# A transformer layer over 32 sequences on one core: another order of the calls in the steady turn and in the outer turns

## The reference

```python
mod = (silu(c) @ wmod).reshape(32, 6, 1, 128)      # sa, ca, ga, sb, cb, gb; ga and gb kept away from 0
h = layernorm(x) * (1 + ca) + sa
h = rmsnorm(h, norm_w)
q, k, v = h @ Wq, split(h @ Wkv)                   # 16 heads of 64, causal softmax over 256 keys
x = x + ga * ((sigmoid(h @ Wg) * softmax(mask(q @ k.T / 8)) @ v) @ Wout)
h = layernorm(x) * (1 + cb) + sb
# product-key experts: 4 heads, 2 x 64 keys, 8 best of each, 8 best of the 8 x 8 pairs, 512 experts
sim = einsum(h @ Wq2, keys); top8 of both halves; softmax over the 8 best pairs
w = silu(h . down_embed[idx]) * softmax; experts = sum(w * up_embed[idx])
mlp = (silu(h @ Wg2 + bg) * (h @ Wu + bu)) @ Wd + bd
x = x + gb * (mlp + experts)
```

## Time and profile before

| what | us |
|---|---|
| three timed runs | 1451.94, 1453.22 (median), 1456.62 |
| the profiled execution's own time | 1454.25 |
| its span, first to last instruction | 1452.5 |
| PE busy | 1400.9 (96%) |
| DVE busy | 1290.8 (89%) |
| ACT busy | 1265.5 (87%) |
| POOL busy | 1052.5 (72%) |

### The profile page before, as it was taken

How to read it: one execution, slowest core, us unless ns; L and a number is a source line. 1 busy time by engine, 2 the same in 40 slices (tenths; PEclk the granted TensorE clock), 3 DMA queues, 4 the chain that set the end, 5 groups by cost and what they waited for, 6 DMA issues and landing times.

```text
span 1452.5 us, 39813 instructions
## 1 busy us (share of the span) xinstructions
PE 1400.9 (96%) x11491; PEld 1163.0 (80%) x11491; DVE 1290.8 (89%) x5345; ACT 1265.5 (87%) x4194; POOL 1052.5 (72%) x1221
## 2 busy tenths in 40 slices
PE   6899999999999999999999999999999999999988
PEld 4678788888788888888888888888878888878868
DVE  6589999999999999999999999999999999999978
...
DMA packets 50753, 27.74 MB, mean 19 GB/s; under 512 B 10304, under 2 KB 49920, under 8 KB 50720
## 3 DMA queue, kind: packets, MB, share of 16 engines
...
...
## 4 chain that ended last, share of the span: by engine, by line
PE 79%; ACT 14%; issue 3%; DVE 2%; DMA 0%; SPq 0%; POOL 0%; ACTq 0%; DVEq 0%; POOLq 0%
PE pW L1381 9%; PE pS L1449 9%; PE pW L1462 9%; PE pW L1490 8%; PE pW L1383 8%; PE pW L1382 8%; PE pS L1439 7%; PE pS L1435 6%; PE pW L1530 4%; PE pW L1533 4%; ACT pS L644 4%; ACT pT L636 4%; PE pW L1466 3%; PE pW L1521 2%; ACT qk L626 2%
## 5 line engine op out<-in xcount | busy, mean ns | idle before, releaser
L644 ACT ACTIVATE pS<-pS,nmx 128x128 f32<-128x128 f32 (+1 forms) x1024 | 388.3, 433 | 34.7 <-DVE nmx L1031 34.7
L501 POOL TENSOR_TENSOR fexp<-fexp,fsum 128x512 f32<-128x512 f32 x240 | 299.8, 1281 | 76.9 <-DVE fexp L1145 76.9
L1031 DVE CUSTOM_DVE_ANT_0 pS<-pS,mask 128x128 f32<-128x128 f32 (+1 forms) x1024 | 331.6, 388 | 25.4 <-PE pS L1439 20.9
L636 ACT COPY pT<-pS 128x768 f32<-128x768 f32 x256 | 215.9, 843 | 40.9 <-PE pS L1449 38.5
L492 POOL TENSOR_TENSOR fsum<-ex 128x512 f32<-128x512 f32 x248 | 250.5, 1048 | 0.0
L1449 PE MATMUL pS<-ident,p_sb 128*128 128x128 f32 x1536 | 215.6, 277 | 5.3 <-DVE p_sb L1051 3.3
L1051 DVE TENSOR_TENSOR p_sb<-pS,coef 128x256 f32<-128x256 f32 (+2 forms) x512 | 210.5, 452 | 8.9
L1449 PEld LDWEIGHTS pS<-ident,p_sb 128*128 128x128 f32 x1536 | 173.3, 140 | 35.8 <-issue 19.6
L644 ACT ACTIVATION_READ_ACCUMULATOR pS<-pS,nmx 128x1 f32 x1024 | 194.7, 190 | 0.0
L626 ACT COPY qk<-pW 128x512 f32<-128x512 f32 x256 | 162.2, 634 | 5.9 <-PE pW L1383 2.3
L1462 PE MATMUL pW<-pT,v 128*64 128x256 f32 x1024 | 165.8, 402 | 0.3 <-ACT pT L636 0.2
...
## 6 DMA issues: line engine op xcount, KB each, us to landing
...
```

Source lines behind the costliest of these rows:

```text
L501: ins = nc.gpsimd.tensor_tensor(fexp[:, k, h, :], fexp[:, k, h, :], fsum[:, k, h].rearrange("p i j -> p (i j)"), ALU.mult)
L636: nc.scalar.copy(pT[:, p % 2], pS[:, p % 2, :, 0:SW]).then_inc(S(pT_ready), 1)
L644: ins = nc.scalar.activation(ps, ps, ACT.Exp, bias=nmx[:, p % 2, h, k:k + 1], scale=-1.0, accum_out=den(p)[:, h, k:k + 1])
L1031: ins = nc.vector.tensor_tensor_reduce(out=ps, in0=ps, in1=mask[:, (1 - k) * P:2 * P], scale=-1.0, scalar=LARGEST, op0=ALU.add, op1=ALU.mi ...
```

## The change

The same work is done in another order, on all engines. In the steady turn:

- PE: the table of banks and the list of calls are new. The turn begins with `project_qk(2)` instead of `project_v(0)`; `project_v(0)`, `project_v(3)` and two `project_qk` follow the first scores; `project_out` moves ahead of `transpose_scores(1)`; the two `project_down` are apart, one on each side of three score calls.
- ACT and DVE: lists to match. `rows2` stands ahead of `copy_transposes(2)`; `choose(1, 0)` follows the first `gate_product`, `choose(0, *)` stays.
- POOL: `add_bias` ahead of `weigh(0)`, `rstd2` ahead of `fold(0)`, `add_heads(1)` ahead of `rstd1`, `fold(1)` ahead of `rms1`.

In the outer turns: the first 256 columns of Wq and of Wkv are loaded first and split apart; the first layernorm's modulation is read straight from PSUM; the transposes of `down_embed` go from the start to the end of turn 0, and POOL splits that weight last; in the last turn the similarities are not shifted by DVE (`shift`), but ACT takes the exponentials from PSUM with the negated maximum as bias (`largest`, `expert_exp_last`), and several calls of the last turn change places.

The diff, cut to the steady lists and what the prediction speaks of:

```diff
...
+            sp.dma_start(w_qkv[:, 0:2 * P], Wq[:, 0:2 * P]).then_inc(load_pairs, 16)
+            sp.dma_start(w_qkv[:, DI:DI + 2 * P], Wkv[:, 0:2 * P]).then_inc(load_pairs, 16)
...
             sp.dma_start(key_sb[:, :, :], keys.rearrange("h k p n -> k h (p n)")).then_inc(load_keys, 16)
-            sp.dma_start(w_qkv[:, 0:DI], Wq).then_inc(load_q, 16)
-            sp.dma_start(w_qkv[:, DI:2 * DI], Wkv[:, 0:DI]).then_inc(load_k, 16)
-            sp.dma_start(down_sb[:, :, :], down.rearrange("(c p) d -> p c d", p=P)).then_inc(load_down, 16)
+            sp.dma_start(w_qkv[:, 2 * P:DI], Wq[:, 2 * P:DI]).then_inc(load_q, 16)
+            sp.dma_start(w_qkv[:, DI + 2 * P:2 * DI], Wkv[:, 2 * P:DI]).then_inc(load_k, 16)
             sp.dma_start(w_qkv[:, GV:GV + H], Wgate).then_inc(load_gv, 16)
             sp.dma_start(w_qkv[:, GV + H:], Wkv[:, DI:2 * DI]).then_inc(load_gv, 16)
+            sp.dma_start(down_sb[:, :, :], down.rearrange("(c p) d -> p c d", p=P)).then_inc(load_down, 16)
             sp.dma_start(w_out[:, :, :], Wout.rearrange("(j p) n -> p j n", p=P)).then_inc(load_w, 16)
             sp.dma_start(w_g[:, :], fWg).then_inc(load_w, 16)
...
@@ -580,16 +587,16 @@
                 candidates()
                 products(0)
                 products(1)
+                add_bias()
                 weigh(0)
-                add_bias()
                 add_heads(0)
+                rstd2()
                 fold(0)
-                rstd2()
                 weigh(1)
+                add_heads(1)
                 rstd1()
-                add_heads(1)
+                fold(1)
                 rms1()
-                fold(1)
             run(pool, body)
...
                             nc.scalar.activation(tops[:, :, :, :].rearrange("p a h n -> p (a h n)"), top_d[:, :, :, :].rearrange("p a h n -> p (a h n)"),
                                                  ACT.Exp).then_inc(S(tops_ready), 1)
+                def expert_exp_last(k):
+                    act.wait_ge(negated, k + 1)
+                    act.wait_ge(S(f_ready[k]), at(f_ready[k], g, 1))
+                    sim = w.bank("sim", k)[:, :].rearrange("p (a h n) -> p a h n", a=2, n=NK)
+                    for a in range(2):
+                        for h in range(RH):
+                            ins = nc.scalar.activation(ex[:, k, a * RH + h, :], sim[:, a, h, :], ACT.Exp, bias=neg[:, a, k * RH + h:k * RH + h + 1])
+                    w.release(ins, "sim", k)
+
+                def tops_exp():
+                    act.wait_ge(S(top_d_ready), at(top_d_ready, f, 1))
+                    act.wait_ge(S(cand_ready), at(cand_ready, g, 1))
+                    nc.scalar.activation(tops[:, :, :, :].rearrange("p a h n -> p (a h n)"), top_d[:, :, :, :].rearrange("p a h n -> p (a h n)"),
+                                         ACT.Exp).then_inc(S(tops_ready), 1)
...
+                queries(2)
                 copy_transposes(7, -1)
-                queries(2)
                 values(0)
+                values(3)
+                exp_scores(0)
                 queries(3)
-                exp_scores(0)
                 weighted(6)
-                values(3)
+                weighted(7)
+                queries(4)
                 gate_up(1)
+                copy_transposes(0, 0)
                 exp_scores(1)
-                weighted(7)
+                values(1)
+                scale_head(1)
+                queries(5)
+                exp_scores(2)
+                copy_transposes(1, 0)
                 down_tanh(0)
-                scale_head(1)
-                copy_transposes(0, 0)
+                total(0)
+                gate_up(2)
+                rows2()
+                weighted(0)
+                copy_transposes(2, 0)
+                exp_scores(3)
+                gate_up(3)
+                scale_head(3)
                 down_tanh(1)
-                copy_transposes(1, 0)
-                gate_up(2)
-                values(1)
-                exp_scores(2)
-                total(0)
-                weighted(0)
-                exp_scores(3)
-                copy_transposes(2, 0)
+                modulate_h()
+                copy_transposes(3, 0)
                 weighted(1)
-                queries(4)
-                scale_head(3)
-                rows2()
-                gate_up(3)
-                queries(5)
-                copy_transposes(3, 0)
-                values(4)
-                modulate_h()
                 high_part(h2T_high, h2T, "hT")
                 exp_scores(4)
                 queries(6)
-                weighted(2)
-                values(2)
+                values(4)
+                experts(0)
                 exp_scores(5)
                 queries(7)
-                values(5)
+                weighted(2)
+                weighted(3)
+                total(1)
                 scale_head(5)
-                weighted(3)
                 copy_transposes(4, 0)
                 copy_transposes(5, 0)
-                total(1)
+                values(2)
+                values(5)
+                expert_exp(0)
+                expert_exp(1)
+                experts(1)
+                rms_scale()
+                exp_scores(6)
                 weighted(4)
-                expert_exp(0)
-                rms_scale()
-                experts(0)
-                expert_exp(1)
                 high_part(xT_high, xT, "xT")
                 weighted(5)
-                experts(1)
-                exp_scores(6)
                 exp_scores(7)
                 gate_up(0)
+                copy_transposes(6, 0)
                 queries(0)
-                copy_transposes(6, 0)
                 scale_head(7)
                 queries(1)
...
+                def largest(k):
+                    w.wait_full("sim", k)
+                    sim = w.bank("sim", k)[:, :].rearrange("p (a h n) -> p a h n", a=2, n=NK)
+                    heads = slice(k * RH, (k + 1) * RH)
+                    apart()
+                    for a in range(2):
+                        for h in range(RH):
+                            ins = nc.vector.max(top_s[:, a, k * RH + h, :], sim[:, a, h, :])
+                    link(ins, head_chain, f)
+                    nc.vector.tensor_scalar(neg[:, :, heads], top_s[:, :, heads, 0], -1.0, None, ALU.mult).then_inc(negated, 1)
+                    if k == TB - 1:
+                        nc.vector.tensor_tensor(top_d[:, :, :, :], top_s[:, :, :, :], top_s[:, :, :, 0:1].broadcast_to([P, 2, TB * RH, TK]),
+                                                ALU.subtract).then_inc(S(top_d_ready), 1)
...
@@ -1300,41 +1370,41 @@
                 row_max(0)
                 choose(0, 0)
                 choose(0, 1)
+                normalise(0)
                 row_max(1)
-                normalise(0)
                 bias_product(1)
                 gate_product(1)
+                choose(1, 0)
                 normalise(1)
+                row_max(2)
+                ln1_stats()
+                ln2_stats()
+                normalise(2)
                 gated_down(0)
-                choose(1, 0)
-                gated_down(1)
-                row_max(2)
                 row_max(3)
                 bias_product(2)
-                normalise(2)
-                ln2_stats()
+                choose(1, 1)
                 gate_product(2)
-                choose(1, 1)
                 normalise(3)
-                ln1_stats()
                 bias_product(3)
                 gate_product(3)
                 row_max(4)
+                gated_down(1)
+                low_part(h2T_high, h2T, "hT")
                 row_max(5)
-                low_part(h2T_high, h2T, "hT")
                 normalise(4)
                 shift(0)
                 normalise(5)
+                shift(1)
                 ln1_modulate()
-                shift(1)
                 row_max(6)
                 row_max(7)
+                normalise(6)
                 low_part(xT_high, xT, "xT")
-                normalise(6)
                 finish()
                 bias_product(0)
+                gate_product(0)
                 normalise(7)
-                gate_product(0)
                 if first:
...
-                project_v(0)
+                project_qk(2)
                 scores(0)
                 transpose_scores(7, -1)
-                project_qk(2)
+                project_v(0)
+                project_v(3)
                 project_qk(3)
-                project_v(3)
+                project_qk(4)
+                weigh_values(6)
+                weigh_values(7)
                 scores(1)
-                weigh_values(6)
                 gate_up(1)
-                weigh_values(7)
+                transpose_scores(0, 0)
+                project_v(1)
+                project_qk(5)
+                scores(2)
+                project_out()
+                transpose_scores(1, 0)
                 project_down(0)
-                project_v(1)
```

(46 more changed lines are left out.)

197 lines of the change are left out of this document (122 added, 75 removed), and 10 rows, old and new, of the table order.

## The result

The changed kernel takes 1470.92 us (median of 4 runs, 1467.83 to 1472.36), the kernel before 1452.58 beside it: ratio 1.0115 (1.0126 from the medians alone), 95% interval 1.0103 to 1.0128. The forecast was 1452, its range ended at 1470. The profiled execution has a span of 1466.05 us against 1452.46, so 13.6 us are to be found in the two traces. The medians are 18.3 us apart: the profiled execution of the changed kernel was the fastest of its four (1467.83, granted clock 0.990, the others 0.986 to 0.988), that of the kernel before was 1.7 over its median. No trace shows where those 4.8 us lie.

What follows compares the result with a forecast made beforehand. PE, busy 42.74 of 43.44 us, was taken as the bound, with DVE and ACT near full. From the profiled 1454.25, +2.9 for steady turns and -4.0 for outer turns gave 1453.2, less 1.0 for the median 1452 us; range 1432 to 1470.

Steps and rivals of the forecast that it cites:

- The outer turns: Start and last turn: -2.5 us at the start, -1.0 and -0.5 in the last turn; sum -4.0, bounds -8 and 0.
- wait of 2.43 us: At the start, PE's wait for the copy of the turned `down_embed`, which moves to the end of the turn.
- the ring of the softmax: In the opening, what replaces PE's wait for the `down_embed` copy, so little of that gain was called sure.
- The third rival: The outer turns bring nothing: PE's clock or the ring takes back what the start won; 1456 us, chance 0.06.
- The steady turn: Each of 29 turn distances: -1.10 + 0.20 + 1.0 = +0.1 us a turn, +2.9 us in all.
- Waits of 1.10: PE's waits at `scores(5)` 0.47, `project_qk(4)` 0.34 and `scores(3)` 0.29 us a turn go: up to -1.10 us.
- the two places named: New PE waits for ACT's copies: `scores(4)` 0.7 us and `scores(5)` 0.3 us, together +1.0 us a turn.
- PE's own steps: On PE, changes between kinds of call have a price; the new order costs +0.20 us a turn, bounds 0 and +0.4.
- term (a): `rows2` ahead of `copy_transposes(2)` on ACT: a 9.7 us chain against PE's 9.0, so `scores(4)` waits 0.7 us, bounds 0.3 and 1.8.
- The lock decides: Rival: `choose(1, 0)` takes 2.4 us or more beside `weigh(0)`, `scores(4)` waits 1.3 us; +0.7 a turn, 1469.5 us, chance 0.28.
- The waits go and do not come back: Rival: quicker `ln2_stats` and `rows2`, only 0.4 us of PE's waits stay; -0.6 us a turn, 1432 us, chance 0.30.
- `project_qk(6)`: Sign of error: PE waiting at its bank, taken as free, for `gate_product(3)`; a few tenths of slack only.

Runs made afterwards that it cites:

- old_lists: The changed kernel with the old table of banks, steady lists and turn 0, keeping the start's and last turn's edits: 1449.47 us, 0.9973 of the kernel before.
- rows_late: The changed kernel with `rows2` directly behind `copy_transposes(2)` on ACT instead of two calls ahead of it: 1475.25 us, 1.0162 of the kernel before.
- ln1_stats_late: The changed kernel with `ln1_stats` on DVE moved behind the low part of `h2T`, one call moved: 1462.39 us, 1.0065 of the kernel before.
- own_banks: The changed kernel, every list kept, with turn 0's 18 projection and weighing jobs in banks dealt round in their own order: 1462.76 us, 1.0072 of the kernel before.

## Why the forecast was wrong, point by point

- **The outer turns** are the step that failed: -4.0 with bounds -8 and 0, measured +8.9 (13.6 less the 4.7 of the 28 turns). Its two terms held where they stand alone: *old_lists* gains 2.3 at the start and 1.5 at the end (forecast 2.5 and 1.5). The first of them is in part luck: the first projection starts 1.62 us sooner there (13.42 for 15.04), as meant, but the rest of the gain lies ahead of the first exponential too, and not in the wait of 2.43 us that I had counted on: turn 0 of *old_lists* is only 0.3 us shorter than before. What I had not costed is that turns 0 and 1 run the new table and lists with much of a turn's work absent. I read turn 0's diff for the transposes that left it and put down "the ring of the softmax" for the rest. Walking the table for turn 0 alone, with its 21 jobs, would have shown `project_qk(2)` and `project_qk(4)` in one bank with only `project_qk(3)` between them, and four more pairs like it. The third rival, 1456, allowed for the start's gain to be eaten, not for a loss.
- **The steady turn** came as forecast: +0.18 us by the distance of `project_out` for +0.1. Waits of 1.10 went, 1.07 came (forecast 1.0, at the two places named, 0.79 and 0.28 for 0.7 and 0.3), and PE's own steps grew from 43.41 - 1.10 = 42.31 to 43.59 - 1.07 = 42.52, +0.21 (forecast +0.20).
- **The reading of term (a)** was right as to the chain and wrong as to the remedy it suggests. *rows_late* shows that `rows2` in front of the copy is not a cost in itself. The chain was priced at 9.7 us and took 738.46 + 0.80 + 0.14 - 729.54 = 9.86. That it fits so well is luck: DVE reached the result 4.35 us after the start of `project_out` and not 3.8, from there to POOL's last factor it took 3.51 and not 3.82, and from there to `scores(4)` 2.00 and not 2.14.
- **"The lock decides"**: `choose(1, 0)` did run beside `weigh(0)`, 2.28 us, and DVE reached `ln2_stats` 4.35 us behind the start of `project_out`, past the 3.8 that the rival named as its point. But the wait came to 0.79, not 1.3. What DVE's lateness is worth, *ln1_stats_late* shows: 0.25 us a turn, 7 us in all. But that run takes `ln1_stats` away and leaves the masks at 2.28 us, and DVE then comes 0.26 us early; so the lateness is that of the long masks and `ln1_stats` together, and no run takes the masks' delay away alone. This rival had the path right, a third of the size, and its cause in part. My reading of the earlier trace rows was rough too: the second mask ended 0.28 us behind POOL's first instruction (719.16 and 718.88 in the single rows), and the first was hardly held up (0.63).
- **"The waits go and do not come back"** had its chance from the idle time of ACT and DVE. Those averages hardly changed (39.07 and 39.17 us busy now); the idle time lies elsewhere in the turn than the stretch from `exp_scores(2)` to `scores(5)`.
- `project_qk(6)` did not wait for its bank. Of the two masks of `choose(1, 0)` one was as long as said (1.49 us), the other took 0.86.

Still open: where the 4.8 us lie by which the medians differ more than the traces; why *own_banks* leaves a clock of 0.82 in turn 0 though PE idles less, and what part of the last turn's gain the new lists give back (0.9 instead of 1.5).
